# An attention entry ordered half a round earlier, maxima in three bank pairs, and one mixer block behind the last products with V

## The reference

```python
x = x + ssm(layernorm(x))        # linear recurrence, gelu, layer norm, gamma/beta, nan_to_num
x = x + ffn(layernorm(x))        # mix with the token before, sigmoid(xr Wr) * (relu(xk Wk)^2 Wv)
x = x + attention(layernorm(x))  # 16 heads of 64, causal, below
x = x + ffn(layernorm(x))

def attention(x):
    latent = x @ w_kv_down                     # rank 128
    k, v = split(latent @ w_kv_up)             # 16 heads of 64 each
    q = x @ w_q
    att = softmax(causal(q k^T * 64**-0.5))
    return (att @ v) @ w_out
```

## Time and profile before

| what | value |
|---|---|
| median of 3 runs | 2120.46 us (2118.05 to 2121.39) |
| the profiled execution | 2122.19 us, its span 2120.8 us |
| busy, share of the span | PE 93%, DVE 63%, ACT 52%, POOL 67% |
| mean granted TensorE clock | 0.977 |

### The profile page before, as it was taken

One profiled execution on the slowest core, in us unless ns is written; L12 is line 12 of the kernel. 1 busy time (PEld: TensorE's weight loads), 2 busy tenths in 40 slices (PEclk: granted clock), 3 DMA queues, 4 the chain that ended last, 5 costly groups with the idle time before them and its releaser, 6 DMA issues.

```text
span 2120.8 us, 34863 instructions
## 1 busy us (share of the span) xinstructions
PE 1974.7 (93%) x12720; PEld 1222.6 (58%) x12720; DVE 1345.3 (63%) x2719; ACT 1098.1 (52%) x2233; POOL 1426.4 (67%) x812
## 2 busy tenths in 40 slices
PE   6998668999999999999989999999999999999898
PEld 4665445555555565555555655555555555555466
DVE  7888556576657666666656657576656575666353
ACT  5775534445444454445455444445445445444575
POOL 1333215778687868787858687868786878687822
PEclk9999689999999999999999999999999999999999
DMA  3000000000000000000000000000000000000001
GB/s 123 1 1 1 0 7 6 20 12 17 12 20 11 17 12 20 19 10 19 13 11 17 11 20 11 17 12 20 12 18 11 20 12 18 11 14 12 26 26 60
DMA packets 29242, 36.99 MB, mean 17 GB/s; under 512 B 6928, under 2 KB 20368, under 8 KB 29072
## 3 DMA queue, kind: packets, MB, share of 16 engines
q1 hardware_dynamic: 29072, 34.76, 5.3%
HBM read 30.02 MB, written 4.46 MB: 16 GB/s over the span
## 4 chain that ended last, share of the span: by engine, by line
PE 60%; DVE 15%; POOL 14%; ACT 6%; issue 4%; DMA 0%; POOLq 0%; ACTq 0%; SPq 0%; DVEq 0%
PE heads_out L881 15%; POOL acc L1377 12%; PE beside L698 9%; PE two_heads L837 7%; PE scores L698 6%; PE scores L860 4%; PE scores L866 4%; PE scores L862 4%; PE scores L864 4%; DVE part_max L1075 3%; ACT prob L1292 2%; PE beside L892 2%; PE two_heads L698 2%; DVE wQK_lo L1036 1%; DVE stats L920 1%
## 5 line engine op out<-in xcount | busy, mean ns | idle before, releaser
L1377 POOL TENSOR_TENSOR acc<-acc,prob 128x1024 f32<-128x1024 f32 (+3 forms) x512 | 1018.3, 1989 | 205.0 <-ACT prob L1292 149.6
L1292 ACT ACTIVATE prob<-scores 128x512 f32<-128x512 f32 (+3 forms) x1280 | 579.6, 539 | 640.1 <-PE scores L866 288.9
L1075 DVE TENSOR_REDUCE part_max<-two_heads 128x2 f32<-128x1024 f32 x384 | 469.4, 1222 | 278.0 <-PE two_heads L837 277.1
L881 PE MATMUL heads_out<-prob,V 128*64 128x512 f32 (+3 forms) x2560 | 544.3, 546 | 0.0
L1072 DVE CUSTOM_DVE_ANT_0 two_heads<-two_heads,mask 128x128 f32<-128x128 f32 (+3 forms) x512 | 242.2, 515 | 187.5 <-PE two_heads L837 187.4
L837 PE MATMUL two_heads<-k_hi,q_hi 64*128 64x512 f32 (+3 forms) x1280 | 274.7, 424 | 62.3 <-DVE part_max L1075 32.5
L881 PEld LDWEIGHTS heads_out<-prob,V 128*64 128x64 f32 x2560 | 156.8, 137 | 233.4 <-issue 210.2
L837 PEld LDWEIGHTS two_heads<-k_hi,q_hi 64*128 64x128 f32 x1280 | 121.1, 185 | 255.4 <-issue 131.3
L860 PE MATMUL scores<-q_hi,k_hi 64*128 64x512 f32 (+3 forms) x1280 | 236.0, 364 | 1.6 <-ACT neg_max L1279 0.8
L866 PE MATMUL scores<-neg_max,sel 64*128 64x512 f32 (+3 forms) x1280 | 235.4, 362 | 0.0
L862 PE MATMUL scores<-q_hi,k_lo 64*128 64x512 f32 (+3 forms) x1280 | 235.3, 362 | 0.0
(11 more groups left out here) (297 smaller groups left out, 2910.8 us busy)
## 6 DMA issues: line engine op xcount, KB each, us to landing
rden<-rden_rows SPq DMA_DIRECT2D x128, 128.0 KB, 2.9
X<-u SPq DMA_DIRECT2D x8, 512.0 KB, 8.6
out<-X SPq DMA_DIRECT2D x8, 512.0 KB, 2.9
wQK_raw<-wQuery SPq DMA_DIRECT2D x16, 192.0 KB, 3.1
wO_raw<-wOut SPq DMA_DIRECT2D x16, 128.0 KB, 2.7
wV_raw<-wValue SPq DMA_DIRECT2D x8, 128.0 KB, 2.9
den<-den_rows SPq DMA_DIRECT2D x64, 4.0 KB
rden_rows<-den SPq DMA_DIRECT2D x64, 4.0 KB, 1.3
```

Of the source, the lines that this page charges most:

```text
L881: made = pe.matmul(heads_out[head(h), x0:], V[vn % NVS][:, tt, p % 2, head(h)], prob[step % NPROB][:, h, x0:], start=t == 0, stop=t == TPB ...
L1075: made = ve.reduce_max(part_max[:, t, :, c:c + 1], two_heads[:, :, 0:width], AX.X)
L1292: ac.activation(prob[step % NPROB][:, h, x0:], bank(task, h)[:, x0:], ACT.Exp).then_inc(empty(task, h)[0], 1)
L1377: po.tensor_tensor(total[:, :, x0:], total[:, :, x0:], new[:, :, x0:], ALU.add).then_inc(acc_ok, 1)
```

## The change

The change has five parts.

1. `ENTRY` brings the entry of the attention forward, by one place at its first task and by most of a round at the later ones. The weights' high parts (`load_pair`, `load_values`) and the first transposes stand at the begin of round 8, ahead of `update a 5`; key 0 and query 0 stand ahead of the products of block 6, the four maxima of unit 0 around them, and key 1, query 1 and the maxima of unit 1 ahead of and around the products of block 7.
2. `attention` becomes a generator that yields after each pair of steps. `first_layers` takes its first two pairs ("pair" in `ENTRY`, round 10): the scores of steps 0 and 1 stand ahead of `update a 7`, the scores of steps 2 and 3 and the first `weigh` behind it, ahead of `first_layers_done`. While the first layers run, only urgent maxima and early fillers are taken.
3. The tiles `prob` and `oT` get other addresses, which `first_layers_done` does not guard; the wait on `x_plus_ssm` moves from `state_space_memory` to the first exponential. On GpSimd the constants of `attention_start` are now written ahead of the last additions of the state space layer.
4. When a maximum directly follows a maximum (with no task that takes a bank and no `weigh` between them), it takes the next of three bank pairs, (5, 6), (0, 1), (2, 3). It happens at eight maxima, all among the units 1 to 4: the last list entry that differs before the end of the kernel is one of them, and between there and the last steps both lists are the same. Also `filler` is called once more behind each maximum of a catch-up.
5. In `ahead`, `mix_tokens b 1` moves from ahead of the scores of steps 12 and 13 of the last unit to behind its last `weigh`. Behind it all banks are given out in turn, two banks further on.

```diff
-ENTRY = {(8, "updated"): [("turn_tiles", 0, 0)], (8, "mixed"): [("turn_tiles", 0, 2)], (8, "tail"): [("latent", 0, 0)],
-         (8, "products"): [("turn_tiles", 0, 4)], (9, "begin"): [("attention_start",), ("load_pair", 0), ("load_values", 0)],
-         (9, "updated"): [("key", 0), ("query", 0)], (9, "mixed"): ["maximum", ("turn_tiles", 0, 6), "maximum", ("value", 0, 0), ("value", 0, 1)],
-         (9, "products"): ["maximum", ("latent", 0, 1), "maximum", ("turn_max", 0)], (9, "end"): [("key", 1), ("query", 1)],
-         (10, "updated"): ["maximum", ("turn_tiles", 0, 8), "maximum", "maximum"]}
+ENTRY = {(8, "begin"): [("load_pair", 0), ("load_values", 0), ("turn_tiles", 0, 0)], (8, "updated"): [("turn_tiles", 0, 2)],
+         (8, "mixed"): [("latent", 0, 0), ("turn_tiles", 0, 4)], (8, "tail"): [("attention_start",), ("key", 0), ("query", 0)],
+         (8, "products"): ["maximum", ("turn_tiles", 0, 6), "maximum", ("value", 0, 0)],
+         (8, "end"): ["maximum", ("value", 0, 1), "maximum", ("turn_max", 0)],
+         (9, "begin"): [("latent", 0, 1)], (9, "updated"): [("key", 1), ("query", 1)], (9, "mixed"): ["maximum", ("turn_tiles", 0, 8), "maximum"],
+         (9, "products"): ["maximum", ("turn_tiles", 0, 10), "maximum"], (9, "end"): ["maximum", ("latent", 0, 2), "maximum"],
+         (10, "begin"): ["pair"], (10, "updated"): ["pair"]}
...
         elif kind == "maximum":
-            self.take(task, (5, 6))
+            before = next((x[0] for x in reversed(self.tasks[:-1]) if x in self.bank or x[0] == "weigh"), None)
+            self.max_banks = (self.max_banks + 1) % 3 if before == kind else 0
+            self.take(task, ((5, 6), (0, 1), (2, 3))[self.max_banks])
...
     def phases(self):
+        self.pairs = self.attention()
         self.first_layers()
-        self.attention()
+        self.add("first_layers_done")
+        self.layers_done = True
+        for _ in self.pairs:
+            pass
...
-                 -6: [("mix_tokens", "b", 1)], -4: [("turn_normal", "b", 2)]}
+                 -4: [("turn_normal", "b", 2)], 0: [("mix_tokens", "b", 1)]}
...
-            goal = min(len(self.maxima), max(urgent, min(s + 2 + LEAD, self.at + 3)))
+            goal = min(len(self.maxima), max(urgent, min(s + 2 + LEAD, self.at + 3))) if self.layers_done else urgent
...
-            if s == 0:
-                self.add("first_layers_done")
...
             while self.at < goal - 1:
                 maximum()
+                filler(10 ** 6)
...
-            w.wait_ge(x_plus_ssm, 2 * NBL)
...
+                    if not step:
+                        w.wait_ge(x_plus_ssm, 2 * NBL)
```

More of the change, by code:

```diff
@@ L75, in __init__ @@
         self.count = [0] * 8
-        self.in_steps, self.done, self.chores = False, set(), []
-        self.side_bank = 7
+        self.in_steps, self.layers_done, self.done, self.chores = False, False, set(), []
+        self.side_bank, self.max_banks = 7, 0
         self.kinds, self.nth, self.masked = {}, {}, {}
@@ L244, in entry @@
                 self.next_maximum()
+            elif task == "pair":
+                next(self.pairs)
             else:
@@ L412, in filler @@
         def filler(latest):
-            open_ = sorted((x for x in fillers if x[0] <= s and x[2] not in self.done), key=lambda x: x[1])
+            open_ = sorted((x for x in fillers if x[0] <= s and x[2] not in self.done and early(x[2])), key=lambda x: x[1])
             if open_ and open_[0][1] <= latest:
@@ L431, in due, with early @@
             return True
-        self.in_steps = True
+        def early(task):
+            return self.layers_done or task[0] in ("turn_tiles", "latent") or task[1] < {"key": 2, "query": 2, "turn_max": 2, "value": 1}.get(task[0], 0)
         for s in range(0, len(steps) + 2, 2):
-            for load in sorted(x for x in loads if x[0] <= s):
+            self.in_steps = True
+            if s == 2:
+                self.heads_free = self.freed[4]
+            for load in sorted(x for x in loads if x[0] <= s and self.layers_done):
                 loads.remove(load)
@@ L475, in attention @@
             self.add_all(ahead.get(s - len(steps), []))
-        self.in_steps = False
+            self.in_steps = False
+            yield
         for n, piece in enumerate(self.last_mixer()):
@@ L519, in full, with two_banks @@
             return filled[b], n
+        def two_banks(task):
+            first = plan.bank[task][0][0][0]
+            return two_heads[:, :, :] if first == 5 else scores[:, first:first + 2, :]
         def empty(task, i=0):
@@ L836, in tensor_program @@
                     for h in range(2):
-                        made = pe.matmul(two_heads[:, h, 0:width], q[head(h), t * P:(t + 1) * P], k[head(h), 0:width], start=True, stop=True)
+                        made = pe.matmul(two_banks(task)[:, h, 0:width], q[head(h), t * P:(t + 1) * P], k[head(h), 0:width], start=True, stop=True)
                     made.then_inc(full(task)[0], 1)
@@ L1071, in vector_program @@
                         for h in range(2):
-                            made = ve.tensor_tensor_reduce(out=two_heads[:, h, 0:width], in0=two_heads[:, h, 0:width], in1=mask[:, BLK - width:], scale=1.0,
-                                                           scalar=MASKED, op0=ALU.add, op1=ALU.max, accum_out=part_max[:, t, h, c:c + 1])
+                            scored = two_banks(task)[:, h, 0:width]
+                            made = ve.tensor_tensor_reduce(out=scored, in0=scored, in1=mask[:, BLK - width:], scale=1.0, scalar=MASKED, op0=ALU.add, op1=ALU.max, accum_out=part_max[:, t, h, c:c + 1])
                     else:
-                        made = ve.reduce_max(part_max[:, t, :, c:c + 1], two_heads[:, :, 0:width], AX.X)
+                        made = ve.reduce_max(part_max[:, t, :, c:c + 1], two_banks(task)[:, :, 0:width], AX.X)
                     made.then_inc(empty(task)[0], 1)
```

5 lines of the change are left out of this document (2 added, 3 removed).

## The result

The changed kernel takes 2132.79 us (median of 4 runs, 2132.57 to 2135.66), the kernel before 2119.26 us beside it (2115.72 to 2121.39): ratio 1.005, 95% interval 1.0029 to 1.0071. It is slower, by about 13.5 us; I had predicted 2122 and a range up to 2129.

A forecast was written before the change was run, and what follows sets the result against it. The prediction took a nearly full TensorE (busy 1974.7 of 2120.8 us) as the bound. Its terms, 3.8 - 8.0 + 3.7 + 3.0 - 0.7 = 1.8 us longer, gave 2122 us beside the median of 2120.46, range 2114 to 2129.

The forecast's parts named there:

- Stage 1: From 201.2 us to the first score, at 289.0 instead of 285.23: 3.8 us longer.
- Stage 2: From there to the first score of unit 1, 28.9 us before, 20.9 predicted: 8.0 us shorter.
- Stages 3 and 4: First score of unit 1 to its step 6 score, 3.7 us longer; then to 383.2 us, 3.0 longer.
- Stage 4's upper bound of 5: From unit 1's step 6 score to 383.2 us: at most 5 us longer, if no value is saved.
- Last steps: Last unit: moving `mix_tokens b 1` removes TensorE's 0.70 wait behind VectorE; 0.7 us shorter, bounds 0.3 and 1.5.
- the 3.10: TensorE's 3.10 us wait for `oT_lo` near the kernel's end, predicted to stay with the low clock behind it.
- The late products of block 7: Entry: products 11.8 us late; `update a 7` at low clock, unit 1's first score 5 us later; 2127, chance 0.22.
- the 314: Sign of the slower rival: first score of unit 1 behind 314 us, or `update a 7` at 7 us.
- GpSimd did not hold `wQK_lo`: Rival before key 0: GpSimd blocks VectorE's `wQK_lo`, key 0 comes 1.8 us later; 2124, chance 0.08.
- The clock held in the entry: Rival: three of four low-clock bursts behind the first key run at 2.4 GHz, saving 6 to 8 us; 2115, chance 0.28.

The follow-up runs named there:

- b_turns: The kernel before with only the banks in turn for neighbouring maxima, nothing else of the change; ratio 1.0025 of before, measured 2127.25 us.

## Why the prediction was wrong, by its steps

- **Stage 1**, predicted +3.8, measured +4.1. Right, place by place.
- **Stage 2**, predicted -8.0, measured -5.6. The mechanism held; the clock was low for nearly all of it (0.73), where I had charged it for part of the stage.
- **Stages 3 and 4**, predicted +3.7 and +3.0, measured +8.8 and +8.5. This is the step that failed: "With banks in turn the second maximum starts at once, but the score, in banks 0 and 1, waits for both reductions: 0.5 + 1.2 + 1.2 = 2.9 from the start of the first, where 1.8 + 0.4 = 2.2 passed before". The wait itself was priced well: the pair at 353.31 has its score at 356.26, 2.95 us later. Over both stages TensorE's idle time grew from 10.4 to 18.7 us, by 8.3 where the terms add up to 6.7. But I priced every matmul there at full clock, since the clock of before was 0.93 and 1.00, and did not ask what the longer waits would do to it: the same 365 matmuls took 66.2 us in place of 57.2. These 9.0 us had no term. The experiments show where they come from: without the turns 10.4 us of the work between units 0 and 2 are gone, and with the same waits filled 10 us come back. Stage 4's upper bound of 5 had no term for it either.
- **Last steps**, predicted -0.7 with bounds 0.3 and 1.5, measured -3.9 in the profile and some 5 us in the timed pair, whose intervals overlap. The mechanism was right; the size came from an execution where a slow `weigh` hid most of the wait. That the 3.10 "stays, and so does the low clock behind it" was half wrong too: in the changed kernel that `weigh` took 1.94 us, and across the profiles this goes either way. The term was mis-sized because I took one row's wait (0.70) and not VectorE's 4.84 less what lay beside it at full clock.
- **Sum:** +4.1 - 5.6 + 8.8 + 8.5 = 15.8, and 16.5 at unit 2's read-out; the stretch to unit 62 was 2.2 faster in this execution, the last unit 3.9: 16.5 - 2.2 - 3.9 = 10.4, the difference of the spans.
- **Rivals.** None came true. The late products of block 7 end on the right side (2127) by the wrong cause: they came where I had put them, and the first score of unit 1 was at 312.55, before the 314 that I had named as its sign. GpSimd did not hold `wQK_lo`: two of them took 0.61 us. The clock held in the entry no better than I had charged. What was missing is a rival in which a stage at full clock loses it.

The Trainium skill has this as a rule, on its page "TensorE: Matmul & The Clock Gate", section "HAM oscillation — how this bites in real kernels": where each tile's work is followed by a wait, the clock drops in the wait and the next tile starts slow, each time anew. The Trainium skill tells it of waits for transfers. The traces here agree, for waits for VectorE, with 0.87 against 1.00 from 347 to 398 us and 10 us over two units. The waits in that example of the Trainium skill are about 3 to 5 us. Here none in the slow stretch is longer than 2.81, and the clock fell all the same.

What stays open: why the new entry takes 5.9 us longer from unit 0 to 2 with no turn in it was read from the waits and not tried piece by piece; and how the clock falls in one execution and not in another in the same place (0.77 and 0.86 from 201 to 243 us in before and b_turns, the same instructions there) no run here settles.

## What to carry to other kernels

A clock of 1.00 in a stretch belongs to the waits that the stretch has now, and can differ by some hundredths from one execution to the next. Where a change makes waits fewer but longer on TensorE, price the matmuls behind them at both clocks, and fill one such wait with needless matmuls to see which share is the clock's. More banks for a producer pay where several of its results stand in a row ahead of one consumer; where every pair is followed by a consumer in those same banks, the wait only moves to the consumer and grows, so give the turned one the banks that are needed last.

## What the runs showed that was not expected

- Needless work made the kernel faster: eight matmuls of no use at each of seven waits, some 2 us for the eight, took the time from unit 0 to 2 from 91.32 to 81.29 us.
- A wait can stand in the profile at 0.70 us and be 3.12 in another execution of the same steps, since TensorE at low clock (3.68 us for what takes 1.94) covers it.
- One execution differs from another by up to 6 us over the same 1590 us of work. Columns by unit tell kernels apart where whole times don't, but each of them has a scatter of up to 3 us of its own.
